# Gated cross-attention and ternary feed-forward: layer norm for four batches at a time, and attention halves summed inside PSUM

## What is computed

```python
def _layernorm(x, axis=-1, eps=1e-05):
    m = jnp.mean(x, axis=axis, keepdims=True)
    v = jnp.var(x, axis=axis, keepdims=True)
    return (x - m) / jnp.sqrt(v + eps)
...
q = (x @ Wq).reshape(B, N, HEADS, hd).transpose(0, 2, 1, 3)
k = (context @ Wk).reshape(B, M, HEADS, hd).transpose(0, 2, 1, 3)
v = (context @ Wv).reshape(B, M, HEADS, hd).transpose(0, 2, 1, 3)
scores = jnp.einsum('bhid,bhjd->bhij', q, k) * scale
attn = jax.nn.softmax(scores, axis=-1)
out = jnp.einsum('bhij,bhjd->bhid', attn, v)
return out.transpose(0, 2, 1, 3).reshape(B, N, DIM) @ Wo
...
h = jax.nn.gelu(jnp.einsum('bsd,fd->bsf', x, _ternary(W1)) + b1, approximate=False)
out = jnp.einsum('bsf,df->bsd', h, _ternary(W2)) + b2
...
x = x + jnp.tanh(g_xattn[0]) * _L0_xattn_ref(_layernorm(x, axis=-1), ctx_768, ...)
x = x + jnp.tanh(g_ffn[0]) * _L0_ffn_ref(_layernorm(x, axis=-1), ...)
```

## Time and profile before

| what | value |
|---|---|
| median of 3 runs | 1853.07 us (1853.0 to 1859.49) |
| span of the profiled execution | 1838.7 us |
| median less span | 14.4 us |
| instructions | 47676 |
| ScalarE busy | 952.2 us, 52% |
| GpSimd busy | 661.2 us, 36% |
| all DMA | 101.13 MB, mean 55 GB/s |

### The profile page before, as it was taken

How to read it: one execution, slowest core, us unless ns; L and a number is a source line. 1 busy time by engine, 2 the same in 40 slices (tenths; PEclk the granted TensorE clock), 3 DMA queues, 4 the chain that set the end, 5 groups by cost and what they waited for, 6 DMA issues and landing times.

```text
span 1838.7 us, 47676 instructions
## 1 busy us (share of the span) xinstructions
PE 1761.7 (96%) x14501; PEld 1152.8 (63%) x14501; DVE 1538.3 (84%) x4375; ACT 952.2 (52%) x1799; POOL 661.2 (36%) x809
## 2 busy tenths in 40 slices
PE   6999999999999999999999999999799999999998
PEld 3666666666666666666666666666466666666665
DVE  6799798898888988888898888987788888888886
ACT  3455555554555555555555555544455555555554
POOL 2344454454444444444444444545211111111111
PEclk9699898898988988898898888987699999999999
DMA  3222222222222222222222222221101110001011
GB/s 98 59 65 74 55 64 68 60 64 69 59 59 59 74 59 59 74 59 59 69 64 59 71 58 59 75 53 36 50 24 35 34 34 31 26 34 34 34 34 47
DMA packets 170607, 101.13 MB, mean 55 GB/s; under 512 B 20817, under 2 KB 170321, under 8 KB 170577
## 3 DMA queue, kind: packets, MB, share of 16 engines
q1 hardware_dynamic: 170576, 100.75, 20.0%
HBM read 32.53 MB, written 16.78 MB: 27 GB/s over the span
## 4 chain that ended last, share of the span: by engine, by line
PE 84%; DVE 8%; issue 5%; ACT 2%; DVEq 0%; DMA 0%; ACTq 0%
PE bank L1059 11%; PE bank L312 10%; PE bank L352 9%; PE bank L328 9%; PE bank L305 8%; PE bank L391 8%; PE bank L296 8%; PE bank L372 5%; PE bank L1089 5%; PE bank L1088 5%; PE bank L373 2%; PE bank L381 2%; DVE smax L759 2%; DVE y L1046 2%; PE bank L285 1%
## 5 line engine op out<-in xcount | busy, mean ns | idle before, releaser
L914 POOL TENSOR_TENSOR probl<-prob 128x512 f16<-128x512 f32 x512 | 531.6, 1044 | 712.5 <-ACT prob L596 710.9
L596 ACT ACTIVATE prob<-bank,masks 128x512 f32<-128x512 f32 x512 | 344.6, 686 | 314.3 <-PE bank L352 301.8
L744 DVE TENSOR_REDUCE smax<-bank 128x4 f32<-128x512 f32 x512 | 348.5, 682 | 46.1 <-PE bank L328 46.0
L1075 DVE TENSOR_TENSOR hidl<-hid 128x512 f16<-128x512 f32 x256 | 226.7, 886 | 79.4 <-ACT hid L1070 78.7
L1059 PE MATMUL bank<-y,w1T 128*128 128x512 f16 x1024 | 263.0, 379 | 29.7 <-DVE y L1046 28.2
L1070 ACT ACTIVATE hid<-bank,b_sb 128x512 f32<-128x512 f32 x256 | 175.8, 687 | 212.2 <-PE bank L1059 205.9
L1088 PE MATMUL bank<-w2T,hid 128*128 128x256 f16 x1024 | 237.4, 273 | 1.4 <-ACT w2T L1003 1.4
L1089 PE MATMUL bank<-w2T,hidl 128*128 128x256 f16 x1024 | 237.4, 273 | 0.0
L1153 POOL TENSOR_TENSOR xres<-xres,b2g 128x1024 f32 (+1 forms) x32 | 75.5, 2361 | 431.3 <-ACT yln L1023 413.4
L328 PEld LDWEIGHTS bank<-k_rows,q_rows 16*128 16x128 f16 x2048 | 120.5, 96 | 160.2 <-issue 128.2
L352 PE MATMUL bank<-q_rows,k_rows 50*128 50x128 f16 x2048 | 216.5, 230 | 0.9 <-DMA q_rows<-smaxT 0.9
(11 more groups left out here) (88 smaller groups left out, 2645.0 us busy)
## 6 DMA issues: line engine op xcount, KB each, us to landing
q_rows<-q SPq DMA_DIRECT2D x384, 64.0 KB, 2.6
k_rows<-k SPq DMA_DIRECT2D x384, 64.0 KB, 2.5
xres<-in_x_dram SPq DMA_DIRECT2D x64, 256.0 KB, 2.8
out_dram<-ystage SPq DMA_DIRECT2D x32, 512.0 KB, 2.9
ctx_sb<-in_ctx_dram SPq DMA_DIRECT2D x64, 192.0 KB, 2.9
q_rows<-smaxT SPq DMA_DIRECT2D x128, 8.0 KB
w_raw<-in_L_ffn_W_dram SPq DMA_DIRECT2D x2, 1024.0 KB, 6.6
prob<-in_L_xattn_Wq_dram SPq DMA_DIRECT2D x1, 256.0 KB, 4.0
```

The costliest lines, as they stand in the source:

```text
L596: act.activation(prob[u][:], st_bank[u % 2][:], ACT.Exp, bias=0.0, scale=masks[g.parity][:, 2 + b:3 + b]).then_inc(exp_done, 1)
L744: dve.tensor_reduce(smax[:, b, u * UH:(u + 1) * UH], sm_bank[u % 2][:].rearrange("p (h j) -> p h j", h=UH), AX.X, ALU.max).then_inc(max_ta ...
L914: pool.tensor_tensor(probl[u][:], prob[u][:], prob[u][:].bitcast(BF16)[:, 1::2], ALU.subtract).then_inc(prob_split, 1)
```

## The change

Three things are done together.

1. **Weighing.** The output of a head is 17 columns (`VH`: 16 values and the sum) instead of 33. Each part of the exponentials is multiplied first by the high values with the ones (17 columns) and then by the low values (16 columns), and all four products are added in the same PSUM columns. 16 heads of 17 columns fit one bank, so a batch has one bank (`pv_bank[b]`) and only its first matmul clears it.
2. **Normalisation.** Once for each batch: one reciprocal over 16 sums, and one multiplication that reads PSUM and writes `attn`. The reduction is gone.
3. **Layer norm.** `norm_x` takes four batches (a half) at a time: its 14 parts are issued in even groups only, on tiles of four columns. `load_x` brings four batches. Scale and shift get a tile of their own, `norm`, and the wait for their readers stands at part 12 instead of part 3.

In the last group, `sum_weights(dve, 1)` now stands between the reciprocal and the normalisation of the last batch.

```diff
-LN_AHEAD = 8
...
+    VH = HD + 1
...
         def weigh(pe, g, b, u):
...
-            if u % 2 == 0 and not (isinstance(n, int) and n == 0):
-
-                pe.wait_ge(norm_read, n * 2 + (half - 1))
+            if u == 0 and not (isinstance(n, int) and n < 2):
+
+                pe.wait_ge(norm_done, n - 1)
             for c in range(UH):
-                o = pv_bank[half][:, (c0 + c) * VC:(c0 + c + 1) * VC]
-                v = v16[g.parity][:, b, u * UH + c, :]
+                h = u * UH + c
+                o = pv_bank[b][:, h * VH:(h + 1) * VH]
                 high = prob[u][:].bitcast(BF16)[:, 2 * c * S + 1:2 * (c + 1) * S:2]
-                pe.matmul(o, high, v, start=True, stop=False)
-                last = pe.matmul(o, probl[u][:, c * S:(c + 1) * S], v, start=False, stop=True)
+                low = probl[u][:, c * S:(c + 1) * S]
+                vh, vl = v16[g.parity][:, b, h, 0:VH], v16[g.parity][:, b, h, VH:VC]
+                pe.matmul(o, high, vh, start=(h == 0), stop=False, skip_group_check=True)
+                pe.matmul(o[:, 0:HD], high, vl, start=False, stop=False, skip_group_check=True)
+                pe.matmul(o, low, vh, start=False, stop=False, skip_group_check=True)
+                last = pe.matmul(o[:, 0:HD], low, vl, start=False, stop=(h == HEADS - 1), skip_group_check=True)
...
-        def norm_x(dve, g, parts):
+        def norm_x(dve, half, parts):
...
-        def read_weighed(dve, n, b, half):
...
-            dve.reciprocal(rsum[:, b, heads], pv[:, :, 2 * HD])
-            dve.tensor_reduce(attn[b][:, heads, :],
-                              pv[:, :, 0:2 * HD].rearrange("p h (two d) -> p h d two", two=2), AX.X,
-                              ALU.add).then_inc(norm_read, 1)
...
+        def sum_weighed(dve, n, b):
+
+            dve.wait_ge(weighed, (n + 1) * UNITS)
...
+            dve.reciprocal(rsum[:, b, :], pv_of(b)[:, :, HD]).then_inc(norm_read, 1)
+
+        def normalise(dve, n, b):
+
+            dve.wait_ge(norm_read, n + 1)
+            dve.tensor_tensor(attn[b][:], pv_of(b)[:, :, 0:HD],
+                              rsum[:, b, :].unsqueeze(2).to_broadcast([P, HEADS, HD]),
                               ALU.mult).then_inc(norm_done, 1)
...
             def norm(i):
                 if left == 0:
 
-                    norm_y(dve, Group(0, 0), ((i - LN_AHEAD) % LN_PARTS,))
-                if i < LN_AHEAD and left >= 4:
-                    norm_x(dve, g4, (i,))
-                if i >= LN_AHEAD and left >= 3:
-                    norm_x(dve, g3, (i,))
+                    norm_y(dve, Group(0, 0), (i,))
+                if g.parity == 0 and left >= 4:
+                    norm_x(dve, g.half + 2, (i,))
...
             if left == 0:
                 sum_weights(dve, 0)
                 add_attention(dve, g.batch(0))
-                read_weighed(dve, g.batch(1), 1, 1)
-                normalise(dve, g.batch(1), 1, 1)
+                sum_weighed(dve, g.batch(1), 1)
                 sum_weights(dve, 1)
+                normalise(dve, g.batch(1), 1)
                 add_attention(dve, g.batch(1))
```

More of the change, by code:

```diff
@@ L166, in bass_gated_cross_attention_ternary_ffn @@
         gates_set = sem("gates_set")
-        x_in = [sem(f"x_in{p}") for p in range(2)]
+        x_in = sem("x_in")
         ctx_loaded = [sem(f"ctx_loaded{p}") for p in range(2)]
@@ L242, in sp_group @@
             scored_before = None if first else held(2 * UNITS * g.n)
-            scored_b0 = held(2 * UNITS * g.n + UNITS)
+            scored_b0 = held((g.n + 3) * (2 * UNITS) - 5 * UNITS)
             max_b1, max_b0 = held(g.batch(1) + 1), held(g.batch(0) + 3)
[L246 to L250, removed]
+            x_past = held(g.half + 3) if g.parity == 1 else None
+            if g.parity == 1 and left >= 6:
+                sp.wait_ge(ln_ready, x_past)
+                load_x(sp, g.half + 3)
             if left >= 3:
@@ L657, in ln_part @@
         def ln_part(dve, i, rows, step, base, ready):
-            n = len(rows)
-            half, y, t, shift = (rstd[:, k, 0:n] for k in range(4))
+            half, y, t = (rstd[:, k, :] for k in range(3))
             if i > 0:
@@ L687, in ln_part @@
             else:
-                last = dve.scalar_tensor_tensor(y, t, 1.5, y, ALU.add, ALU.mult)
+                last = dve.scalar_tensor_tensor(norm[:, 0, :] if i == LN_PARTS - 2 else y, t, 1.5, y, ALU.add,
+                                                ALU.mult)
             last.then_inc(step, 1)
@@ L692, in row_of @@
             return xres[:, bass.ds(batch, 1), :].rearrange("p o d -> p (o d)")
-        def norm_x(dve, g, parts):
+        def norm_x(dve, half, parts):
             for i in parts:
                 if i == 0:
-                    dve.wait_ge(x_in[g.parity], 16 * (g.half + 1))
-                if i == 3 and not (isinstance(g.half, int) and g.n == 0):
-                    dve.wait_ge(ln_done, 2 * g.n)
-                rows = [row_of(g.batch(b)) for b in range(2)] if i == 0 else (None,) * 2
-                ln_part(dve, i, rows, ln_step, g.n * (LN_PARTS - 1), ln_ready)
+                    dve.wait_ge(x_in, 16 * (half + 1))
+                if i == LN_PARTS - 2 and not (isinstance(half, int) and half == 0):
+                    dve.wait_ge(ln_done, QB * half)
+                rows = [row_of(half * QB + b) for b in range(QB)] if i == 0 else ()
+                ln_part(dve, i, rows, ln_step, half * (LN_PARTS - 1), ln_ready)
         def low_q(dve, g):
@@ L1010, in norm_y @@
             for i in parts:
-                if i == 3 and not (isinstance(g.half, int) and g.n == 0):
-                    dve.wait_ge(y_done, QB * g.n)
-                rows = [row_of(g.n * QB + b) for b in range(QB)] if i == 0 else (None,) * QB
+                if i == LN_PARTS - 2:
+                    if isinstance(g.half, int) and g.n == 0:
+                        dve.wait_ge(ln_done, B)
+                    else:
+                        dve.wait_ge(y_done, QB * g.n)
+                rows = [row_of(g.n * QB + b) for b in range(QB)] if i == 0 else ()
                 ln_part(dve, i, rows, y_step, g.n * (LN_PARTS - 1), y_ready)
```

117 lines of the change are left out of this document (53 added, 64 removed).

## The result

The changed kernel takes 2218.72 us (median of 4 runs, 2210.98 to 2225.07) against 1853.03 us for the kernel before (4 runs, 1840.95 to 1859.49): ratio 1.199, 95% interval 1.194 to 1.205. The forecast was 2264 us, with a range of 1940 to 2450. The profiled execution has a span of 2213.6 us, 374.9 us more than before.

What follows compares the result with a forecast made beforehand. The prediction took TensorE and its clock as the bound: +403 us for 60 groups, +7 for the other four, +2 at the end, +412 on the 1838.7 us span, plus 14.4 from span to median, gave 2264 us; range 1940 to 2450.

Steps and rivals of the forecast that it cites:

- What bounds the kernel: Whole kernel: TensorE is 84% of what ended last, VectorE 8%; the clock in the attention stage decides.
- VectorE's saving: Attention stage: VectorE loses about 300 us, 5 us a group, worth only what TensorE waited for.
- The starts: Weighing: narrow matmuls start 25 ns apart despite fewer columns, so 64 more cost 1.6 us a group.
- 19.67 us for a group: Attention stage: length of a full-clock group after the change, 18.07 + 1.60 us.
- TensorE waits for it only at the transposes of the maxima: Attention stage: TensorE's only waits for VectorE, 12.9 us in 34 waits, 0.3 us in every second group.
- The clock: Attention stage: share at 1.2 GHz rises from 0.20 to 0.65, a group lasts 26.6 us, +403 us.
- So the falls follow runs of short matmuls, not pauses: Earlier trace: before a fall TensorE was busy 4.75 of 5.1 us; hence a fall expected in nearly every group.
- I return all of it: Attention stage: the 0.3 us wait of TensorE for VectorE in every second group would go entirely.
- the rival on VectorE: VectorE's relief is absent or worth more; dismissed as worth at most TensorE's waits; no chance of its own given.
- The clock never falls: Rival, attention stage: more instructions without a pause hold the clock up; -4 us, 1849 us; chance 0.06.
- By columns: Rival, weighing: narrow matmuls cost by their columns, so the change is faster, 1845 us down; chance 0.05.
- The clock falls no more than now: Rival, attention stage: share at 1.2 GHz 0.10 to 0.35, 1899 to 2043 us; chance 0.19.

Runs made afterwards that it cites:

- before_yield: Kernel before, with only GpSimd's subtraction made to wait until the maxima are rounded; 1755.91 us, ratio 0.946 to 0.956 to the kernel before.
- weigh17: Kernel before with only the new weighing and normalisation (17 and 16 columns), layer norm still of two batches; 1907.57 us, ratio 1.025 to 1.037.
- double33: Kernel before with each 33-column weighing matmul issued twice, output unchanged; 1824.53 us, ratio 0.981 to 0.989 to the kernel before.
- after32: Changed kernel with each narrow matmul widened to 32 columns, the further sums unused; 1881.08 us, ratio 1.010 to 1.018 to the kernel before.
- wide56: Kernel before with each weighing matmul widened from 33 to 56 columns, the further sums unread; 1764.57 us, ratio 0.951 to 0.963.
- after_yield: Changed kernel with only GpSimd's subtraction made to wait until the maxima are rounded; 1996.91 us, ratio 1.078 to 1.089 to the kernel before.
- droplow: Changed kernel without the two matmuls on the low part of the values, which its output lacks; 1900.38 us, ratio 1.022 to 1.033 to the kernel before.
- norm4: Kernel before with only the layer norm changed to four batches at a time, old weighing kept; 1877.7 us, ratio 0.986 to 1.000.

## Why the prediction was right, and where not

**What bounds the kernel: right.** TensorE's stream and its clock set the end. VectorE's saving was put at 300 us and is 300.4 (1538.3 to 1237.9), and it bought nothing here; VectorE needs 12.3 us a group (740.93 / 60), forecast about 12. Its wait for TensorE in line 747 has grown to 357.5 us.

**The starts: right, but 19.67 us for a group was too high.** The starts lie 25 ns apart with 16, 17, 32 and 33 columns; the Trainium skill, "TensorE: Matmul & The Clock Gate", section "Wait — 56ns, not 53.3ns?", states that they come no closer than that, and the trace agrees for the four widths. I took 64 x 25 ns = 1.60 us a group. At full clock the distances between the starts of the weighings add up to 1.52 us a group in before_yield and to 3.15 us in weigh17: 1.63 us more. The group grows only from 18.0 to 19.4 us, because TensorE had a second wait that I missed. In the kernels with the old weighing its transposition of the context (line 285) stands behind the residual addition, and starts 0.44 us after the matmul ahead in before_yield (0.46 us in the kernel before), against 0.22 us in weigh17 and double33. The longer weighings cover this wait. The profile lists it with the weight loads and puts half of the times down to the residual addition; waits of before_yield, then of weigh17, which has none for the addition, 100 to 1150 us:

```profile
PEld bank L285 <- DVE xres L789: 12.3, 29, 0.4
```

```profile
PEld bank L286 <- issue: 3.3, 17, 0.2
```

So "TensorE waits for it only at the transposes of the maxima" was not right either: about 0.27 us a group was waiting that the change took away. The groups at full clock have a mean of 18.16 us in the kernel before and of 19.36 us in weigh17, so 60 x 1.20 = 72 us of the loss are longer groups at full clock: 97 us of starts, less some 24 us of the two waits. (The changed kernel has no group at full clock, so weigh17 stands in for it.)

**The clock: right in size, for a partly wrong reason, and with some luck.** Forecast: share 0.65, group 26.6 us, +403 us. Measured: 0.61, 26.04 us, +366. The rest of the 366 us, 294, is the clock. A microsecond at 1.2 GHz loses (1562 - 60 x 19.36) / 960 = 0.42 us, forecast 0.40. The forecast share was one fall a group of 17 us; the runs have 46 falls in 60 groups, of 20.5 us on average, and fewer and longer falls came to nearly the same. Outside the 60 groups it is 374.9 - 366.0 = 8.9 us, forecast 9. (The forecast's own terms, 1838.7 + 412 + 14.4, add up to 2265 us, not 2264.)

The step that failed is the reading of the earlier trace rows: "So the falls follow runs of short matmuls, not pauses". The row says 4.75 busy of 5.10 us. The missing 0.35 us is the wait for the maxima, 0.4 us ahead of the fall, and I passed over it. By these runs few columns and a short pause bring the falls together: wider matmuls took most of them away with the pauses left in (after32, wide56), and so did taking the pause away with the columns left as they were (before_yield). Neither explains all: weigh17 and after_yield fall without a pause. Since I took the falls to follow the short matmuls alone, I made the weighing alone responsible and gave weigh17 a loss like that of both parts; it had 3%.

The second failed step is "I return all of it", of the 0.3 us wait, and the claim behind it that VectorE's relief is worth only what TensorE waits. The wait stayed, as a gap of 0.2 us in about one group of four, because the layer norm now issues all its parts in even groups and GpSimd's subtraction catches the rounding. The list of waits shows almost nothing of it (0.3 us for line 338 between 100 and 1150 us). Taking it away was worth 222 us. The same holds for the rival on VectorE, "it can't be worth more than TensorE's waits": 13 us of waits held 86 us.

**The rivals.** "The clock never falls": refuted, although TensorE has no gaps in weigh17, whose clock is 0.87. "By columns": refuted by the starts, 25 ns apart, and by droplow, whose group at full clock is no shorter. "The clock falls no more than now" (share 0.10 to 0.35) is what each part alone gives: 0.26 in weigh17, 0.25 in norm4.

## What to carry to other kernels

In a kernel that TensorE bounds, read the granted clock by stretch before counting instructions, and price a short wait of TensorE by what the clock does behind it, not by its length: here 13 us of waits held 86 us, though in after32 the removal of 29 late transpositions gave only 12. Where starts lie 25 ns apart whatever the width (16 to 33 columns here), splitting a matmul into narrower ones doubles its price, while widening it (to 56 columns, even with some that nobody reads) costs a nanosecond and kept the clock up. And a tiny VectorE operation that TensorE waits for should not meet a long one of GpSimd; one semaphore wait on the idle engine was enough here.

## What the runs showed that I had not expected

- More matmuls made the kernel faster: 4096 duplicates, 1.5% less time (double33), because the clock stayed at 1.00 for all but 10.2 us of the 60 groups.
- The time is not a sum of parts: +3% and about 0 gave +20%, through the clock. The pattern repeats with the groups (105.8 us for four, again and again), and some kernels scatter: norm4 took 1830 to 1896 us in ten runs, double33 1816 to 1828.
- An operation on 16 elements took 1.02 us instead of 0.17 when GpSimd's of 1.04 us had started 0.05 us before.
- TensorE's waits by the list were not all its waits: a quarter of a microsecond a group, ahead of the transposition of the context, stood in no row of its matmuls and showed only in the distances between starts.
